# Reordering one tile's work on four engines of a Mamba-2 mixer followed by a quantised feed-forward

## What is computed

```python
proj = einsum('bsd,ed->bse', x, in_proj_w)            # gate 8192 | hs 8192, B 1024, C 1024 | dt 128
hBC = silu(causal_conv4(hBC) + conv_b)                # 4 taps along the tokens
dt = clip(softplus(dt + dt_bias), 0, 100); A = -exp(A_log)
# 128 heads of 64, 8 groups (16 heads each) that share B and C, chunks of 128 tokens
Y_diag = einsum('bzlhn,bzshn,bhzls,bzshp->bzlhp', Cc, Bc, L, xch)      # L = exp(segsum(dt * A))
Y_off  = einsum('bzlhn,bzhpn,bhzl->bzlhp', Cc, prev, exp(A_cum))
g = (Y_diag + Y_off + hs * D) * silu(gate)
out = (g * rsqrt(mean over the group of g*g + eps)) * norm_w
x = x + out @ out_proj_w.T
x = x + w2(silu(w1(n)) * w3(n))                       # n = layernorm(x); 512 -> 1792 -> 512, block-quantised
```

## Time and profile before

| | |
|---|---|
| median of 3 runs | 1877.3 us (1875.56 to 1877.73) |
| the profiled execution | 1877.94 us, its span 1876.1 us |
| PE busy | 1750.3 us, 93% of the span |
| DVE busy | 1263.9 us, 67% |
| POOL busy | 1184.9 us, 63% |
| ACT busy | 840.9 us, 45% |
| DMA | 107.23 MB, 57 GB/s on average |
| granted TensorE clock | 0.992 of full speed |

### The profile page before, as it was taken

One profiled execution on the slowest core, in us unless ns is written; L12 is line 12 of the kernel. 1 busy time (PEld: TensorE's weight loads), 2 busy tenths in 40 slices (PEclk: granted clock), 3 DMA queues, 4 the chain that ended last, 5 costly groups with the idle time before them and its releaser, 6 DMA issues. The chain is left out here.

```text
span 1876.1 us, 34372 instructions
## 1 busy us (share of the span) xinstructions
PE 1750.3 (93%) x10392; PEld 1407.7 (75%) x10392; DVE 1263.9 (67%) x1892; ACT 840.9 (45%) x1273; POOL 1184.9 (63%) x873
## 2 busy tenths in 40 slices
PE   6899999999999999999999989999999998999998
PEld 5677787778777877787778777787778776788886
DVE  7777647772787287736874677557854774977776
ACT  4555345543564355535653555345634553322221
POOL 3487658865777568846775588558765777632430
PEclk9899999999999999999999999999999998999999
DMA  2322102210222022202230222012210221111101
GB/s 95 92 64 85 41 29 80 85 46 22 68 80 68 0 79 85 74 0 73 69 94 3 57 80 84 19 51 67 81 40 29 80 75 42 46 57 34 45 23 45
DMA packets 71341, 107.23 MB, mean 57 GB/s; under 512 B 16740, under 2 KB 25060, under 8 KB 71304
## 3 DMA queue, kind: packets, MB, share of 16 engines
q1 hardware_dynamic: 70296, 105.38, 18.8%
q10 hardware_dynamic: 1008, 1.38, 0.2%
HBM read 103.51 MB, written 3.15 MB: 57 GB/s over the span
## 5 line engine op out<-in xcount | busy, mean ns | idle before, releaser
L794 PE MATMUL proj<-xhi,w_hi 128*128 128x512 f32 x1080 | 447.2, 414 | 80.8 <-DVE gate L1116 76.9
L796 PE MATMUL proj<-xhi,w_lo 128*128 128x512 f32 x1080 | 423.7, 392 | 0.0
L795 PE MATMUL proj<-xlo,w_hi 128*128 128x512 f32 x1080 | 423.6, 392 | 0.0
L794 PEld LDWEIGHTS proj<-xhi,w_hi 128*128 128x128 f32 x1080 | 203.1, 188 | 174.7 <-DVE gate L1116 101.7
L1097 DVE SCALAR_TENSOR_TENSOR v<-proj,par_sb,v 128x510 f32<-128x510 f32 x378 | 279.9, 742 | 72.5 <-ACT v L590 51.7
L492 POOL TENSOR_TENSOR g_lo<-gated,g_hi 128x512 fp32r<-128x512 f32 x128 | 164.0, 1284 | 198.4 <-ACT g_hi L723 198.3
L427 POOL TENSOR_TENSOR w_lo<-w_raw,w_hi 128x512 fp32r<-128x512 f32 x144 | 182.5, 1286 | 138.0 <-ACT w_hi L568 138.0
L796 PEld LDWEIGHTS proj<-xhi,w_lo 128*128 128x128 f32 x1080 | 203.3, 188 | 45.0
L795 PEld LDWEIGHTS proj<-xlo,w_hi 128*128 128x128 f32 x1080 | 203.8, 189 | 35.7
L467 POOL TENSOR_TENSOR gated<-hs,gate 128x512 f32 (+1 forms) x128 | 190.0, 1506 | 51.0 <-DVE hs L1222 51.0
L590 ACT ACTIVATE v<-proj,par_sb 128x512 f32<-128x512 f32 x126 | 97.8, 776 | 248.4 <-PE proj L796 248.4
(11 more groups left out here) (164 smaller groups left out, 3360.4 us busy)
## 6 DMA issues: line engine op xcount, KB each, us to landing
w_raw<-in_win SPq DMA_DIRECT2D x144, 256.0 KB, 4.2
fade_l<-faded SPq DMA_DIRECT2D x128, 256.0 KB, 3.7
wo_raw<-in_wout SPq DMA_DIRECT2D x64, 256.0 KB, 2.6
M<-in_w SPq DMA_DIRECT2D x14, 512.0 KB, 3.8
row_r<-rows SPq DMA_DIRECT2D x256, 3.0 KB
row_l<-rows SPq DMA_DIRECT2D x256, 3.0 KB
cb<-in_w SPq DMA_DIRECT2D x7, 512.0 KB, 3.3
out<-resid SPq DMA_DIRECT2D x8, 256.0 KB, 2.0
```

The source lines that it names most:

```text
L794: e.matmul(o, hi_l, hi_r, start=first, stop=False)
L795: e.matmul(o, hi_l, lo_r, start=False, stop=False)
L796: return e.matmul(o, lo_l, hi_r, start=False, stop=last)
```

## The change

No instruction is added or removed. On SP, `load_pair` moves from the end of a step to its start. On ACT, the scaling of the output weights moves ahead of the second `tap3`, their upper part ahead of `hs_tanh` of half 0, and `gate_tanh` of half 0 ahead of `exponential` of half 0. On DVE, `gate_silu` of half 0 moves ahead of both `weigh_own`, and `hs_silu` of half 0 stands behind the second of the three taps instead of behind the first.

```diff
--- before.py
+++ after.py
@@ -333,6 +333,8 @@
             load_rows(0, 0)
 
             def step(g, j, par_, nxt, nxt2, ahead):
+                if nxt2:
+                    load_pair(9 * g + j + 3, split.at(g, j, 0))
                 sp.wait_ge(wolo.sem, wolo.at(g, j, 0))
                 sp.dma_start(wo_raw[:, :], wout[TPG * g + j, :, :]).then_inc(woraw.sem, 16)
                 if nxt:
@@ -340,8 +342,6 @@
                     load_rows(TPG * g + j + 1, 1 - par_)
                     sp.wait_ge(pdone.sem, pdone.at(g, j, 1))
                     load_fade(TPG * g + j + 1)
-                if nxt2:
-                    load_pair(9 * g + j + 3, split.at(g, j, 0))
 
             def window(g, nxt):
                 if nxt:
@@ -680,28 +680,29 @@
                 if nxt2:
                     act.wait_ge(ready.sem, ready.at(g, j, 0))
                     upper_pair(par_, 9 * g + j + 3)
-                if nxt:
-                    tap3(1, w, ready.at(g, j, 2), silu.at(g, j, 0))
-                    act.wait_ge(gdone.sem, gdone.at(g, j, 0))
-                    hs_tanh(hs[:, 1 - par_, :], 0, taken.at(g, j, 1))
                 act.wait_ge(woraw.sem, woraw.at(g, j, 16))
                 act.wait_ge(gused.sem, gused.at(g, 0, 0))
                 e.activation(wo_raw[:, :], wo_raw[:, :], ACT.Copy,
                              scale=par_sb[:, bass.ds(TPG * g + j, 1), K + 2:K + 3].rearrange("p a b -> p (a b)"))\
                     .then_inc(woscaled.sem, 1)
+                if nxt:
+                    tap3(1, w, ready.at(g, j, 2), silu.at(g, j, 0))
                 act.wait_ge(woscaled.sem, woscaled.at(g, j, 1))
                 e.copy(wo_hi[:, bass.ds(j, 1), :].rearrange("p a f -> p (a f)"), wo_raw[:, :])\
                     .then_inc(wohi.sem, 1)
+                if nxt:
+                    act.wait_ge(gdone.sem, gdone.at(g, j, 0))
+                    hs_tanh(hs[:, 1 - par_, :], 0, taken.at(g, j, 1))
                 if ahead:
                     bounded(g, j + 1, 0)
                 if nxt:
                     hs_tanh(hs[:, 1 - par_, :], 1, taken.at(g, j, 2))
                 if ahead:
                     bounded(g, j + 1, 1)
-                    exponential(g, j + 1, 0)
                 if nxt:
                     gate_tanh(gate[:, 1 - par_, :], 0, ready.at(g, j, 3))
                 if ahead:
+                    exponential(g, j + 1, 0)
                     exponential(g, j + 1, 1)
                 if nxt:
                     gate_tanh(gate[:, 1 - par_, :], 1, ready.at(g, j, 4))
@@ -1087,7 +1088,7 @@
             e.tensor_scalar(par_sb[:, :, 0:K + 1], par_sb[:, :, 0:K + 1], 0.5, None, ALU.mult).then_inc(s_halved, 1)
             e.tensor_scalar(parbc_sb[:, :, :, :], parbc_sb[:, :, :, :], 0.5, None, ALU.mult).then_inc(s_halved, 1)
 
-            def conv_rest(h, weights, ntap, nconv, between=(), banks=proj):
+            def conv_rest(h, weights, ntap, nconv, between=None, banks=proj):
 
                 dve.wait_ge(tap.sem, ntap)
                 dst, src = per_batch(v[:, h, :]), per_batch(banks[h][:, :])
@@ -1097,8 +1098,8 @@
                     e.scalar_tensor_tensor(dst[:, :, d:S], src[:, :, 0:S - d], weights(K - 1 - d),
                                            dst[:, :, d:S], ALU.mult, ALU.add)\
                         .then_inc(taken.sem if d == K - 1 else convs.sem, 1)
-                    if d <= len(between):
-                        between[d - 1]()
+                    if d == 2 and between:
+                        between()
 
             def tile_weights(t):
                 return lambda k: par_sb[:, bass.ds(t, 1), k:k + 1].rearrange("p a b -> p (a b)")
@@ -1214,7 +1215,7 @@
                 if nxt:
                     conv_rest(0, w, tap.at(g, j, 1), convs.at(g, j, 0))
                     conv_rest(1, w, tap.at(g, j, 2), convs.at(g, j, 2),
-                              (lambda: hs_silu(hs[:, 1 - par_, :], 0, tanh.at(g, j, 1)),))
+                              lambda: hs_silu(hs[:, 1 - par_, :], 0, tanh.at(g, j, 1)))
                 own = tile_weights(t)
                 for h in range(2):
 
@@ -1223,11 +1224,9 @@
                                            ALU.mult, ALU.add).then_inc(ysum.sem, 1)
                 if nxt:
                     hs_silu(hs[:, 1 - par_, :], 1, tanh.at(g, j, 2))
+                    gate_silu(gate[:, 1 - par_, :], 0, tanh.at(g, j, 3))
                 if ahead:
                     weigh_own(g, j + 1, 0)
-                if nxt:
-                    gate_silu(gate[:, 1 - par_, :], 0, tanh.at(g, j, 3))
-                if ahead:
                     weigh_own(g, j + 1, 1)
                 if nxt:
                     gate_silu(gate[:, 1 - par_, :], 1, tanh.at(g, j, 4))
```

## The result

The changed kernel takes 1773.38 us (median of 4 runs, 1773.12 to 1775.57) against 1876.71 us (4 runs, 1875.56 to 1877.73): a ratio of 0.9452, 95% interval 0.9436 to 0.9469, 103.3 us less. Forecast were 1779.5 us and 97.8 us less, in a range of 1768 to 1812. Its profiled execution took 1773.44 us, with a span of 1771.6 us.

What follows compares the result with a forecast made beforehand. PE bounds the kernel, idling each tile in a ring through DVE; removing 0.91 and 1.13 us takes the period from 17.12 to 15.25. Savings of 87.9, 5.0 and 4.9 us make 97.8: 1779.5 us, range 1768 to 1812.

Steps and rivals of the forecast that it cites:

- the bound: PE, busy 93% of the span, sets the time; its own work is 15.12 us a tile against a period of 17.12.
- the ring: xdt, DVE's chain, `gate_silu` of half 0, `unit(0)`, `turn`, xdt again: 17.12 us a turn, to become 15.08.
- The sum: Ring 17.12 - 0.91 - 1.13 = 15.08 us, period taken as 15.25; 97.8 us less in all, giving 1779.5 us.
- The pair loaded ahead: SP issues the `w_raw` pair right after POOL's split, so DVE's 0.91 us wait for `tap3` goes; moved-past loads cost nothing.
- rival 2: Only half works: 1819 us if the pair still came late, 1834 if the gate were late; chance 0.06.
- The gate ahead of the wide products: On DVE, `gate_silu` of half 0 goes ahead of `weigh_own`, taking 1.13 us a tile out of the ring.
- ACT's part: `gate_tanh` moved ahead of an `exponential` comes some 0.9 us sooner; without this DVE would wait 0.2 us.
- The covers named: Slack for the delayed `weigh_own`: PE's y needs both products near 725.2 and begins at 730.7, over 3 us to spare.
- `hs_silu` one tap later: On DVE, `hs_silu` of half 0 behind the second tap: nothing in the ring longer, 0, between -0.1 and +0.1 us a tile.
- Rival 1: POOL's work lengthens DVE's `hs_silu`: 1797 us, 1812 at a 15.8 us period, up to 1834; chance 0.15 above the forecast range.
- Rivals 3 and 4: 3: wait moves to POOL, period stays, chance 0.02. 4: PE's granted clock falls, 1909 us at 0.85, chance 0.03.

## Why the prediction was right, and where it was not

**The bound and the sum.** Right in the mechanism of the bound: PE's work gives the period, plus a little where the ring is longer. Right in the number, but in part by luck. The sum has two terms, the load and the gate, and the kernel with these two alone takes 1799.17 us, 20 us over the forecast; that is inside the whole range but outside the 1768 to 1795 that had 0.70: `hs_silu` of half 0 then takes 1.59 us in the median where the sum had it unchanged, 1.19 in its tile. What brought the kernel to 1773 was a move that the sum has at nothing. With it the ring is even a little under the sum in most tiles: from the start of xdt to the end of `gate_silu` it was 13.00 us before, 13.00 - 0.91 - 1.13 = 10.96 by the sum, and 690.61 - 680.03 = 10.58 measured where `hs_silu` took 0.85 us; where it took 1.70 the ring is the longer of the two.

Against the sum's parts: 15.25 was forecast and 15.21 measured, in the full tiles 1.91 us off each. A tile j = 0 gained 15.83 - 14.94 = 0.89 us instead of 0.63: its `hs_silu` of half 0 takes 0.68 to 0.69 us in both kernels, and PE's work alone is its period; the end of a group gained 76.45 - 75.90 = 0.55 instead of 0.7. Six middle groups together went from 1170.90 us (xdt at 270.24 to 1441.14) to 1093.04 (254.80 to 1347.84), 12.98 us each where the sum had 12.55. Between the two profiled executions lie 1877.94 - 1773.44 = 104.5 us, 6.7 more than forecast: 6 x 0.43 = 2.6 in these groups, 0.9 in the last (10.83, where the sum had 9.98), 1.4 up to the first tile's xdt, 1.5 in the first group (14.03) and 0.4 elsewhere. In the opening the rows of the two kernels differ in the granted TensorE clock (us, busy by engine, PEclk, DMA share, GB/s), first before, then after:

```profile
66.00:75.00 9.00, 8.40 (x31) 6.40 (x32) 6.34 (x6) 4.54 (x5) 2.36 (x1) 0.62 0.46 129
```

```profile
66.00:75.00 9.00, 8.42 (x37) 6.41 (x37) 8.02 (x9) 6.19 (x8) 3.96 (x3) 0.81 0.50 144
```

It is 0.62 and 0.81 in the same stretch, so some of its time was at the lower level of 1.2 GHz in both. Whether the change has a part in that was not tried. Part of the 1.4 us is the difference between two executions: the first xdt starts at 72.65 and at 73.11 us in two of the changed kernel, and at 74.21 us in the run with the pair behind the row loads.

**The pair loaded ahead.** The size was right in the changed kernel (DVE's wait fell by 51.5 us), the reading was not complete. The step that failed is the one behind rival 2: "If the pair still came late the period would be 17.12 - 1.13 = 15.99 and the time 1877.3 - 47 x 1.13 - 5 = 1819". It is 1880, and with the rest of the change 1904. I had read the 0.91 us as a wait inside one ring. It was the meeting point of two rings; the second (`w_raw`, `w_hi`, `tap3`, taps, y sum, `gated`, `weigh_past`, `fade_l`, `w_raw`) set the pace, and so the load is the condition of all other gains, not one term among two. Alone it brought 70 us where 48 were expected. The rows held its pieces: 3.03 us of ACT's waiting for the landing, and an issue 9.7 us behind POOL's split; I did not follow what had delayed the issue back to DVE's y sum.

**The gate ahead of the wide products.** Sized at 1.13 us a tile. Added to the early load it brings some 10 us (7 by the two ratios), 15.88 - 15.70 = 0.18 us a tile, since at the shorter period `hs_silu` of half 0 goes from 0.69 to 1.59 us and takes most of it back. With the other two moves as well the kernel is at 1773. The changed kernel with the gate alone undone was not run, so its share there is not known. ACT's part was sized at 0.2 us and is 0.2 us a tile (10 us of the whole), but most of that comes by POOL, as said at that run. The covers named held: PE has no wait for `weigh_own` anywhere.

**`hs_silu` one tap later, and the output weights ahead.** Wrong: "nothing in the ring is longer ... I take 0, between -0.1 and +0.1 us a tile". Undone alone, the tap costs 26 us, 0.5 us a tile. The output weights' place was not undone alone. I priced the instruction as it stood in the order and not by what runs on POOL when it starts. It was the first rival's mechanism, and of the rival I asked only if it would cost the change something, not if a part of the change was there to avoid it.

**Rival 1, DVE held up by POOL.** True as a mechanism, and present in the changed kernel in one of six tiles (1.70 us, period 15.51) and in tile j = 7 (1.73 us). With the squares on ACT it goes, and 10 us with it. It did not cost the forecast its number only because the tap had been moved. `hs_silu` of half 1 takes 1.40 to 1.62 us in every run, while POOL makes `gated`; no run moved that one. By the Trainium skill, page "SBUF — State Buffer", section "SBUF: two separate sides", GpSimd and a VectorE instruction with two SBUF inputs take turns at one pair of ports, the first keeping it for its whole instruction. The rows agree: `hs_silu` ended 0.54 to 0.55 us behind the end of the POOL instruction that had begun before it in all four tiles shown (654.87, 548.74, 712.92 and 511.87 us), and a `wo_lo` that began beside it took 1.73 to 1.75 us instead of 1.29.

**Rivals 3 and 4** did not come: POOL is busy 1201.1 us with no wait of PE on it in the tiles, and the granted clock in the six tiles from 633.96 to 725.22 us is 1.00.

## What to carry to other kernels

Before two waits are added up, follow each back until it comes to itself. Where they belong to different rings, only a repair of the ring that sets the pace gives anything, and the other's counts only after it: here the gate gave nothing alone (1880 us) and the load 70 us (1809). A load's place in its queue is part of such a ring if a wait for late work stands ahead of it; it is enough to put the load ahead of that one wait. And where a VectorE instruction with both inputs in SBUF can meet GpSimd's work, when it starts against the other engine's instructions matters as much as its place in its own engine's order: here 26 us hung on one tap.

## What the runs showed of the hardware

- A SCALAR_TENSOR_TENSOR of 128x512 with both inputs in SBUF takes 0.68 us alone and up to 1.84 us beside POOL (the longest in the changed kernel when it was measured again); the same form with one input in PSUM (`gate_silu`) takes 0.67 to 0.69 us in all runs, also beside POOL's `gated`. POOL's TENSOR_TENSOR of that size goes from 1.29 to a median of 1.74 us in the changed kernel. The time held up counts as busy time of the instruction, not as idle.
- Which of the two goes first differs from tile to tile, but in an order that comes back: `hs_silu` of half 0 takes 0.68, 0.76, 1.70, 1.18, 0.85, 0.92, 0.68 and 1.73 us in the tiles j = 0 to 7 of one middle group of the changed kernel, and within 0.03 us of that in all groups but the last. In the second profiled execution two groups differ: there tile j = 6 has 1.84 us and tile j = 7 has 1.16.
- The pair's median time from issue to landing fell from 4.2 to 2.7 us:

```profile
w_raw<-in_win SPq DMA_DIRECT2D x144, 256.0 KB, 4.2
```

```profile
w_raw<-in_win SPq DMA_DIRECT2D x144, 256.0 KB, 2.7
```

 Before, it was issued right behind the two loads of `fade_l`; in the run with the pair just ahead of them it is 2.7 us too. That the two loads are the reason was not tested by itself.
